# Last cross attention: the values product in two runs, the totals and the inversion moved ahead, the key sums folded

## The reference, cut to what matters

```python
q = split_heads(x @ Wq)                       # 8 batches, 16 heads, 256 queries, 64
k, v = split(context @ Wkv)                   # 1601 keys of 64 for each head
k, v = concat(null_k, k), concat(null_v, v)   # 1602 keys
attn = softmax((q * 64 ** -0.5) @ k.T)
out = concat_heads(attn @ v) @ Wout           # then a layer norm, added to x
```

## Time and profile before

| | us |
|---|---|
| median of 3 runs | 4730.3 (4728.58 to 4740.04) |
| the profiled execution, its own time | 4738.15 |
| its span in the trace | 4736.4 |
| PE busy in the span | 3983.3 |
| DVE, ACT, POOL busy | 3134.0, 2378.4, 1435.4 |

### The profile page before, as it was taken

One profiled execution on the slowest core, in us unless ns is written; L12 is line 12 of the kernel. 1 busy time (PEld: TensorE's weight loads), 2 busy tenths in 40 slices (PEclk: granted clock), 3 DMA queues, 4 the chain that ended last, 5 costly groups with the idle time before them and its releaser, 6 DMA issues. The chain is left out here.

```text
span 4736.4 us, 74916 instructions
## 1 busy us (share of the span) xinstructions
PE 3983.3 (84%) x28530; PEld 2432.5 (51%) x28530; DVE 3134.0 (66%) x5291; ACT 2378.4 (50%) x4528; POOL 1435.4 (30%) x1157
## 2 busy tenths in 40 slices
PE   3399999899199984888877999999999999999754
PEld 2133333388033333666664566666666666666442
DVE  3499998634377736333333678787787778788757
ACT  2288888643099851332321555555555555555330
POOL 0200000000300001111100466666666666666510
PEclk9599999899589986777778999999999999999877
DMA  5322222100355300000001000000000000000001
GB/s 165 66 47 49 49 44 44 23 16 16 55 81 79 58 2 27 0 0 0 0 8 42 15 15 1 15 1 15 1 15 1 15 1 15 1 1 1 5 17 34
DMA packets 119701, 123.09 MB, mean 26 GB/s; under 512 B 21264, under 2 KB 97648, under 8 KB 118992
## 3 DMA queue, kind: packets, MB, share of 16 engines
q1 hardware_dynamic: 119240, 118.27, 11.9%
q10 hardware_dynamic: 144, 0.52, 0.0%
HBM read 103.02 MB, written 15.73 MB: 25 GB/s over the span
## 5 line engine op out<-in xcount | busy, mean ns | idle before, releaser
L835 DVE TENSOR_REDUCE att_peak.1<-psS 128x1 f32<-128x512 f32 (+1 forms) x1024 | 580.3, 631 | 95.8 <-PE psS L705 95.7
L2498 POOL TENSOR_TENSOR key_sums_0.1<-key_sums_0.1,prob_0.1 128x512 f32<-128x512 f32 x256 | 402.6, 1573 | 28.7 <-POOL key_sums_0.1 L2498 0.4
L804 ACT ACTIVATE att_probT.1<-psT 128x512 f32<-128x512 f32 (+1 forms) x682 | 368.8, 568 | 74.8 <-PE psT L734 33.4
L2498 POOL TENSOR_TENSOR key_sums_1.1<-key_sums_1.1,prob_1.1 128x512 f32<-128x512 f32 x256 | 386.8, 1511 | 28.7 <-POOL key_sums_1.1 L2498 0.4
L2337 ACT COPY prob_0.1<-psS 128x1024 f32<-128x1024 f32 (+1 forms) x224 | 203.7, 954 | 323.0 <-PE psS L2236 323.0
L835 DVE TENSOR_REDUCE att_peak.2<-psS 128x1 f32<-128x512 f32 (+1 forms) x512 | 266.8, 568 | 139.4 <-PE psS L705 137.5
L2337 ACT COPY prob_1.1<-psS 128x1024 f32<-128x1024 f32 (+1 forms) x224 | 203.8, 954 | 296.4 <-PE psS L2236 296.4
L705 PE MATMUL psS<-key_stack.1,query_stack.1 64*128 64x512 bf16 (+1 forms) x1024 | 272.2, 387 | 94.4 <-DMA key_stack.1<-key_parts 48.2
L751 PE MATMUL psM<-att_probT.1,quad_values.1 128*9 128x256 f32 (+1 forms) x3840 | 306.3, 391 | 19.5 <-issue 19.5
L2407 DVE TENSOR_TENSOR att_highest.1<-att_highest.1,prob_1.1 128x1024 f32<-128x1024 f32 (+1 forms) x160 | 280.8, 1755 | 53.5 <-ACT prob_1.1 L2337 46.4
L2407 DVE TENSOR_TENSOR att_highest.1<-att_highest.1,prob_0.1 128x1024 f32<-128x1024 f32 (+1 forms) x160 | 271.6, 1698 | 56.6 <-ACT prob_0.1 L2337 49.9
(11 more groups left out here) (681 smaller groups left out, 8936.3 us busy)
## 6 DMA issues: line engine op xcount, KB each, us to landing
key_stack.1<-key_parts SPq DMA_DIRECT2D x384, 58.0 KB
key_stack.2<-key_parts SPq DMA_DIRECT2D x96, 200.1 KB
ctx_rows.1<-in_ctx_dram SPq DMA_DIRECT2D x8, 1536.0 KB
key_parts<-split_parts.1 SPq DMA_DIRECT2D x8, 1200.8 KB, 5.7
ctx_keys_0.1<-in_ctx_dram SPq DMA_DIRECT2D x4, 768.0 KB
ctx_keys_1.1<-in_ctx_dram SPq DMA_DIRECT2D x4, 768.0 KB
query_stack.1<-query_parts SPq DMA_DIRECT2D x192, 16.0 KB
ctx_values_0.1<-in_ctx_dram SPq DMA_DIRECT2D x4, 768.0 KB
```

Of the source, the lines that this page charges most:

```text
L804: last = self.k.nc.scalar.activation(probs[:, blks[0]:blks[-1] + 1, :].rearrange("p b q -> p (b q)"), bank[0:w, 0:len(blks) * S], ACT.Exp)
L835: self.k.nc.vector.tensor_reduce(self.peak[:, 2 * h + s, c:c + 1], self.score_bank[m % 3][:, 0:w], AX_X, ALU.max).then_inc(self.peak_done. ...
L2498: nc.gpsimd.tensor_tensor(acc, acc, own[:, h, c * BANK:(c + 1) * BANK], ALU.add).then_inc(self.summed.sem, 1)
```

## The change

`MEETS` sets which chunks meet in which round: 0 to 3 at the head of round 0 and 4 to 6 at the head of round 2, none in rounds 1 and 3. The total moves from the end of round 2 to its head, ahead of meet 4. POOL gets a seventh instruction for each head, the fold, which adds the second half of `acc` to the first (128 x 256), so that the total needs 2 products in place of 4. On DVE the invert moves ahead of raise 4 and raise 5. The counts of the semaphore `summed` follow (14 for a turn in place of 12).

```diff
@@ -2085,6 +2085,7 @@
     CHUNKS = (KB + 1) // 2
     NULL = KTAIL + 1
     KEYS = KB * P
+    MEETS = [range(0, 4), (), range(4, 7), ()]
 
     def __init__(self, k, mem):
         self.k = k
@@ -2167,7 +2168,7 @@
             sig.passed(T)
         for sig in (self.lowered, self.exped):
             sig.passed(8 * T)
-        self.summed.passed(12 * T)
+        self.summed.passed(14 * T)
         for sig in (self.totalled, self.inverted, self.out_done):
             sig.passed(T)
 
@@ -2259,13 +2260,12 @@
 
     def pe_total(self, pe, i):
         nc = self.k.nc
-        pe.wait_ge(*self.summed(12 * (i + 1)))
+        pe.wait_ge(*self.summed(14 * (i + 1)))
         if i + 1 < self.TURNS:
             pe.wait_ge(*self.lowered(8 * (i + 2)))
-        for part in range(2):
-            for h in range(2):
-                last = nc.tensor.matmul(self.peaks[h * self.HD:(h + 1) * self.HD, 0:S], self.ones[:], self.acc[i % 2][:, h, part * S:(part + 1) * S],
-                                        start=(part == 0), stop=(part == 1))
+        for h in range(2):
+            last = nc.tensor.matmul(self.peaks[h * self.HD:(h + 1) * self.HD, 0:S], self.ones[:], self.acc[i % 2][:, h, 0:S],
+                                    start=True, stop=True)
         last.then_inc(self.totalled.sem, 1)
 
     def pe_meet(self, pe, i, s):
@@ -2291,8 +2291,10 @@
         for i in range(-1, T + 3):
             scores, softmax, meets = 0 <= i < T, 0 <= i - 1 < T, 0 <= i - 2 < T
             for g in range(4):
+                if meets and g == 2:
+                    self.pe_total(pe, i - 2)
                 if meets:
-                    for s in self.of_run(g):
+                    for s in self.MEETS[g]:
                         self.pe_meet(pe, i - 2, s)
                 if softmax and g == 0:
                     self.pe_turn_peak(pe, i - 1)
@@ -2306,8 +2308,6 @@
                 for name in self.due(i, 2 * g + 1):
                     if name is not None:
                         self.pe_project(pe, name)
-                if meets and g == 2:
-                    self.pe_total(pe, i - 2)
 
 
 
@@ -2332,7 +2332,7 @@
         act.wait_ge(*self.scored(g + 1))
         if i >= 2:
             act.wait_ge(*self.met(g - 2 * self.CHUNKS + 1))
-            act.wait_ge(*self.summed(12 * (i - 2) + 6 + max(s, 1)))
+            act.wait_ge(*self.summed(14 * (i - 2) + 7 + max(s, 1)))
         at, w = s * BANK, len(self.of_chunk(s)) * S
         nc.scalar.copy(self.prob[i % 2][:, :, at:at + w], k.psS[:, 2 * (g % 2):2 * (g % 2) + 2, 0:w]).then_inc(self.kept.sem, 1)
 
@@ -2468,11 +2468,11 @@
                 self.dve_raise(dve, i, 3)
             self.dve_take_at(dve, i, 3)
             self.dve_take_at(dve, i, 4)
+            if meets:
+                self.dve_invert(dve, i - 2)
             if scores:
                 self.dve_raise(dve, i, 4)
                 self.dve_raise(dve, i, 5)
-            if meets:
-                self.dve_invert(dve, i - 2)
             self.dve_take_at(dve, i, 6)
             if meets:
                 self.dve_divide(dve, i - 2)
@@ -2486,7 +2486,7 @@
         nc = self.k.nc
         own, acc = self.prob[i % 2], self.acc[i % 2][:, h, :]
         done = 8 * i + 4 * h
-        summed = 12 * i + 6 * h
+        summed = 14 * i + 7 * h
         pool.wait_ge(*self.exped(done + 1))
         if i >= 2 and h == 0:
             pool.wait_ge(*self.totalled(i - 1))
@@ -2500,6 +2500,8 @@
         pool.wait_ge(*self.summed(summed + 5))
         tail = acc[0:self.NULL, 0:S]
         nc.gpsimd.tensor_tensor(tail, tail, own[0:self.NULL, h, 6 * BANK:6 * BANK + S], ALU.add).then_inc(self.summed.sem, 1)
+        pool.wait_ge(*self.summed(summed + 6))
+        nc.gpsimd.tensor_tensor(acc[:, 0:S], acc[:, 0:S], acc[:, S:2 * S], ALU.add).then_inc(self.summed.sem, 1)
 
     def pool_run(self, pool):
         for i in range(self.TURNS):
```

## The result

| | median us | runs |
|---|---|---|
| before | 4735.17 | 4 (4728.58 to 4740.17) |
| after | 4773.42 | 4 (4766.32 to 4775.41) |

The ratio is 1.0079, with a 95% interval of 1.0063 to 1.0096: 38 us more. The forecast was 4764, +33.5 on the median shown then; its range and its sign hold.

What follows compares the result with a forecast made beforehand. PE was taken to bound plain turns before, DVE's block after. Plain +21.1, context +9.0, out -2.1 and end +5.5 make +33.5 us; on the median 4730.3 that is 4764 us (4752 to 4778; 8 in 10: 4728 to 4789).

Steps and rivals of the forecast that it cites:

- What bounds: Plain turn before: PE's own work sets its 27.67 us without gaps; DVE's divide ends only 0.49 before the next meet.
- The block 1.88 later, the wait at the total: Meets 2 and 3 ahead of the turn delay DVE's block 1.88 us; PE stands 0.77 at the total for the lowers.
- The raises behind the invert: Raises 4 and 5 on DVE, both slowed by POOL's sums, take 4.39 us; plain turn 28.31, +0.64.
- the 96 (64 x 1.5) that I had as a sign: Sign of being right: POOL's busy time up by 64 x 1.5 us.
- PE does the same work: Two runs of meets leave PE's work unchanged; only what hangs on it starts 1.88 us later.
- a reckoned 27.22: Plain turn of the faster rival, lowers in time: 27.67 - 0.45 us, 4702 us in all; chance 0.14.
- The out turns: 7 turns with out: PE saves 0.45, DVE's later chain takes part back; -0.3 us each, -2.1 in all.
- Context turns: 21 turns with context transposes: v2 waits for DVE, 1.88 later; 30.45 for 30.02 us, +0.43 each, 9.0 in all.
- the slower rival: Granted clock falls in more than the last turns, or every raise meets POOL: beyond +48, 4785 us and up; chance 0.12.
- The end: Last turn with scores and next iteration: DVE's block 1.88 later in each, two folds more; together +5.5 us.
- The 1.74 that I had added for two more folds: Part of the end's +5.5: two more folds on POOL in the chain to the last total, 1.74 us.
- the +22 of my own lower end: Sum by the terms' lower ends: 10.6 + 9.0 - 3.2 + 5.5 = +22 us.

Runs made afterwards that it cites:

- the kernel with both edits: Changed kernel with the total behind v2 and DVE's take of context or out between raise 2 and raise 3: ratio 0.9868 to the kernel before.
- the kernel without the fold: Changed kernel with six sums a head and a total of 4 products, no fold: ratio 1.0054 to the kernel before.
- the kernel with four rounds: Changed kernel with the meets back in their four old rounds, rest of the change kept: ratio 0.9927 to the kernel before.

## Why the prediction was right, point by point

- *What bounds.* Right: PE with DVE half a us behind. The fold alone shows it: with PE 0.45 shorter and the divide later, the turn was DVE's at once. The Trainium skill (Perfetto Trace Analysis, Identifying the Most-Contended Engine) has TensorE's headroom judged by the share of weight loads, among others, and not by matmul busy time. By that share, 66%, a shorter total would win nothing, as the prediction said apart; here it was worth 27 us once the waits at the total and at the divide were gone.
- *The block 1.88 later, the wait at the total.* Right in kind. The lowers end at 15.95 in place of the forecast 16.11, and the wait is 0.99 where I had 0.77, since PE is faster than I reckoned. Putting the total behind v2 took the wait away and 1.37 from each plain turn.
- *The raises behind the invert.* Right: 4.38, by the argument about where POOL's sums stand: its run of four starts at 3347.20, and raise 4 at 3347.38, 0.18 behind it, where I had 0.16. The plain turn was forecast at 28.31 and came at 28.15, +13.3 in all for +21.1. The Trainium skill (GPSIMD Engine Reference, Specifications) says that GpSimd and VectorE contend where a VectorE instruction has two SBUF inputs; the 4.38 fits it, and the 3.71 in the kernel with both edits shows again that it need not cost both raises so much. POOL pays as well: its busy time rose by 121 us, not by the 96 (64 x 1.5) that I had as a sign.
- *"PE does the same work".* This step failed. Four meets in one run take 3.60 (3324.18 to 3327.78) where two runs of two took 2 x 1.88 = 3.76, meets 4 to 6 take 2.29 (3340.73 to 3343.02) for 2.42, and the keys that are no longer followed by meets or the total shorten by 0.09 each. Without waits a plain turn is 26.77 for a reckoned 27.22. The out turns, which wait for nothing, show it: -1.08 each, forecast -0.3.
- *Context turns.* Mis-sized: +1.05 each for +0.43, 22.0 us for 9.0. The mechanism was right as far as it went: turns that kept the clock are longer by 0.15 (the first two of a batch) and 0.4 (the third). What was missing is the clock: 11 turns with 1.6 us each, 17.6 of the 22. I had it as the slower rival's cause and argued against it with the 1.36 of waiting that did no harm; 2.0 us of waiting did. (That rival's bound was also mis-added: +48 on 4730.3 is 4778, not 4785.)
- *The end.* Mis-sized: +5.5 forecast, +10.1 measured. There too the idle stretches grew and cost clock. Timeline of PE in the last turn with scores and at the next:

```profile
4451.21 1.12 PE L2267 MATMUL psO<-key_sums_1.1,att_ones.1 128*64 128x256 f32 x4 [3.78 <-DVE prob_0.1 L2428]
...
4464.59 5.21 PE L2282 MATMUL psT<-prob_0.1,values_0.1 128*64 128x256 f32 x32 [4.04 <-DVE att_outT.3 L2442]
```

  The total takes 1.12 for the 0.65 it has elsewhere and the meets 5.21 for 3.67: PE came back slow twice, where the earlier trace rows had it once. It did so a third time in the turn behind, where the total, which had waited for nothing there before, stood 6.09 us for the lowers and the three meets behind it took 3.75 for 2.36. The 1.74 that I had added for two more folds does not show: the last total starts at 4494.11, right behind its meets, and waits for no sum.

So the sum was near because errors offset each other, which is luck: plain and out turns together lost 13 us less than forecast, since PE's runs are faster; context turns and the end lost 18 us more, most of it by the clock. Without the 17.6 us of the falls in the context turns the block would have lost some 20 us by my estimate, less than the +22 of my own lower end.

## What to carry to other kernels

Before moving work forward on one engine, list what hangs on the instructions that it is moved past: here the peak's transposes, and through them the other engine's longest unbroken block. Judge each part by what bounds when it stands alone and when the waits are gone; the fold was +0.22% alone and -0.56% in the best version, where the invert's new place was worth 2.0%. And when a large change loses, look for the wait before giving it up: two edits of a few lines, neither of which touches the arithmetic, turned +0.79% into -1.32%.

## What the runs showed of the hardware

- Two waits of the same length, 2.01 and 2.03 us after the same kind of work, left TensorE at 1.2 GHz in one turn and at 2.4 GHz in the next. Of 14 such turns 11 fell. The fall costs 1.6 us, nearly as much as the wait. No fall followed the 14 waits of 1.56 to 1.60 in the kernel without the fold. The length alone does not decide: with the total behind v2 the clock fell after all seven waits of 2.88, after six of seven of 2.40, but after only two of seven of 2.50. What decides was not found.
- Matrix products that fill half the array (128*64) seem to cost a little each time PE changes between them and full ones (128*128). With the same products, and no wait of PE over 0.1 us in either, the plain turns of the kernel with four rounds take 27.23 at the least and those of the kernel with two runs and both edits 26.76. That it is the change of form was not tried by itself.
- The fold, 128 x 256 with both inputs in SBUF, takes 0.73 us on POOL in the median of the changed kernel, and up to 1.59. What it cost when tried alone was not its own length but the shift of POOL's sums behind it, which took two raises on DVE from 3.57 to 4.39 us.
